# An expert-choice MoE and LoRA layer pair on one core: threshold search with seven candidates a step, one-hots built with a scalar per partition, and other work moved around them

## The reference

```python
w = weights[subjects]                              # layer 0, conditioning
flat_x = jnp.einsum('bct,bcd->bdt', x, w).reshape(N, D)
logits = flat_x @ Wg + bg
top_vals, top_idx = jax.lax.top_k(logits, 2)
probs = softmax(sparse top-2 logits)
for i in range(4):
    assigned = (top_idx == i).any(axis=-1)
    score = jnp.where(assigned, probs[:, i], -jnp.inf)
    sel_p, sel_idx = jax.lax.top_k(score, 1024)    # expert choice
    h = jax.nn.gelu(flat_x[sel_idx] @ W1[i], approximate=False)
    out = out.at[sel_idx].add(h @ W2[i] * sel_p[:, None])
x = x + out
x = x + layer1(x)        # silu(gate) * up with LoRA, down, then the scaled linear layer
```

## Time and profile before

| what | us |
|---|---|
| median of 3 runs (651.81 to 652.7) | 651.91 |
| the profiled execution, whole | 653.1 |
| its span in the trace | 651.3 |

### The profile page before, as it was taken

One profiled execution on the slowest core, in us unless ns is written; L12 is line 12 of the kernel. 1 busy time (PEld: TensorE's weight loads), 2 busy tenths in 40 slices (PEclk: granted clock), 3 DMA queues, 4 the chain that ended last, 5 costly groups with the idle time before them and its releaser, 6 DMA issues.

```text
span 651.3 us, 9696 instructions
## 1 busy us (share of the span) xinstructions
PE 605.0 (93%) x3323; PEld 503.4 (77%) x3323; DVE 382.1 (59%) x827; ACT 214.4 (33%) x448; POOL 132.6 (20%) x113
## 2 busy tenths in 40 slices
PE   4867389999999999979999999999999999999994
PEld 2735269999999999967888888888888888888883
DVE  7687867886786556505455545554555455545533
ACT  2435025764874755432212213122122131221110
POOL 4000040745453540652002003011030020000000
PEclk9979579999999999999999999999999999999997
DMA  8996329416329330831003104013031040120012
...
DMA packets 64219, 60.74 MB, mean 93 GB/s; under 512 B 37424, under 2 KB 56624, under 8 KB 62832
## 3 DMA queue, kind: packets, MB, share of 16 engines
...
...
## 4 chain that ended last, share of the span: by engine, by line
PE 86%; DVE 7%; DMA 2%; issue 1%; ACT 1%; POOL 0%; SPq 0%; ACTq 0%; DVEq 0%; POOLq 0%
PE bank L1081 23%; PE bank L1082 22%; PE bank L1083 22%; PE bank L1293 5%; PE bank L1262 3%; PE bank L1260 3%; DVE mix_row L668 2%; PE bank L1140 1%; PE bank L1114 1%; PE bank L1147 1%; PE bank L1194 1%; DVE onehot_r L831 1%; PE bank L1254 1%; DVE passed L780 1%; DVE passed_n L783 1%
## 5 line engine op out<-in xcount | busy, mean ns | idle before, releaser
L621 ACT ACTIVATE act<-bank 128x512 f32<-128x512 f32 x64 | 38.2, 598 | 229.9 <-PE bank L1293 229.9
L1046 DVE TENSOR_TENSOR prod<-bank,act 128x512 f32<-128x512 f32 x64 | 44.2, 690 | 99.6 <-PE bank L1293 99.6
L957 DVE TENSOR_TENSOR hid_lo<-hf,hid_hi 128x512 fp32r<-128x512 f32 (+1 forms) x72 | 45.4, 631 | 48.6 <-ACT hf L567 48.2
L1081 PE MATMUL bank<-w_hi,hid_hi 128*128 128x256 f32 x256 | 72.2, 282 | 0.0
L1082 PE MATMUL bank<-w_lo,hid_hi 128*128 128x256 f32 x256 | 72.1, 282 | 0.0
L1083 PE MATMUL bank<-w_hi,hid_lo 128*128 128x256 f32 x256 | 71.5, 279 | 0.0
L452 POOL DMA_INDIRECT x_rows<-y_sb,slot_row x32 | 53.7, 1678 | 65.9 <-ACT y_sb L554 58.9
L564 ACT ACTIVATE hid_hi<-bank 128x512 fp32r<-128x512 f32 (+1 forms) x72 | 39.8, 552 | 71.1 <-PE bank L1083 70.7
...
L1081 PE MATMUL bank<-xs_hi,w_hi 128*128 128x512 f32 (+1 forms) x144 | 54.7, 380 | 0.0
L1082 PE MATMUL bank<-xs_lo,w_hi 128*128 128x512 f32 (+1 forms) x144 | 53.2, 370 | 0.0
L1083 PE MATMUL bank<-xs_hi,w_lo 128*128 128x512 f32 (+1 forms) x144 | 53.2, 370 | 0.0
...
## 6 DMA issues: line engine op xcount, KB each, us to landing
...
xT<-in_xT SPq DMA_DIRECT2D x8, 512.0 KB, 8.5
x_sb<-in_x SPq DMA_DIRECT2D x8, 512.0 KB, 8.7
flat_rows<-flat_st SPq DMA_DIRECT2D x8, 512.0 KB, 5.5
outT<-out_sb SPq DMA_DIRECT2D x120, 32.0 KB, 1.6
...
```

Of the source, the lines that this page charges most:

```text
L621: act.activation(act1[h % 2][:, :], bank[h % 2][:, :], ACT.Silu).then_inc(silu1, 1)
L957: dve.tensor_tensor(lo[:, n], hf[s % 2][:, n], hi[:, n].bitcast(f32), ALU.subtract).then_inc(hid0, 1)
L1046: dve.tensor_tensor(prod[h % 2][:, :], bank[2 + h % 2][:, :], act1[h % 2][:, :], ALU.mult).then_inc(prod1, 1)
L1081: pe.matmul(out, lh, rh, start=start, stop=False, skip_group_check=True)
```

## The change

- **Masks and copies.** mix_row begins as a copy of adapter 0's matrix in place of the memset; seven predicated copies follow, and the z masks of quarters 0 and 1 stand between them, that of quarter 2 behind them, that of quarter 3 behind the copies into mix. PE's order of products, transposes and logits is changed to match.
- **Search.** Ten steps of three bits: seven candidates per expert. The comparison is two halves of 16 columns (448 elements each), each with its own count of asked. The sum over the columns on VectorE is gone: PE adds four slices of eight columns into one region of 224 columns, and VectorE sums the eight that are left, from PSUM.
- **Items.** Sixteen ahead of the search (twelve before), then two per step for eight steps and one per step for two; the last three folds come behind `route(0)`, in place of the eight fillers. WAIT_PARTS0 falls from 6 to 3.
- **ACT.** The casts of the first expert's weights to w_hi stand behind item 31 instead of item 22, and the Gelu table is loaded behind item 33.
- **One-hots.** onehot_r is written by eight tensor_scalars of 128 elements per quarter, each with a column of pos_r (now f32) as its scalar per partition. VectorE no longer waits for all items ahead of them (wdT has moved to other memory).

```diff
@@ -19,7 +19,8 @@
-SEARCH_STEPS = 15
+SEARCH_STEPS, SEARCH_BITS = 10, 3
+CAND = 2 ** SEARCH_BITS - 1
@@ -153,7 +154,7 @@
-        pos_r, pos_q = sb("pos_r", [P, E, G], bf16), sb("pos_q", [P, E, G], bf16)
+        pos_r, pos_q = sb("pos_r", [P, E, G], f32), sb("pos_q", [P, E, G], bf16)
@@ -179,9 +180,9 @@
-        cursor[0] = onehot_at
+        cursor[0] = offset_of["xs1_hi"]
...
-        assert cursor[0] <= late_at
+        assert cursor[0] <= hid_at
@@ -210,10 +211,10 @@
-        cand = sb("cand", [P, E, 3], f32)
-        passed = sb("passed", [P, E, 3, G], bf16)
-        passed_n = sb("passed_n", [P, E, 3], bf16)
-        kept = [sb(f"kept{i}", [P, E, 4], f32) for i in range(2)]
+        cand = sb("cand", [P, E, CAND], f32)
+        passed = sb("passed", [P, E, CAND, G], bf16)
+        passed_n = sb("passed_n", [P, E, CAND], f32)
+        kept = [sb(f"kept{i}", [P, E, CAND + 1], f32) for i in range(2)]
@@ -311,8 +312,7 @@
-        ROWS_BEFORE_SPLITS = 22
-        ROWS_FIRST = 12
+        ROWS_FIRST, FOLDS_LATE = 16, 3
@@ -327,7 +327,7 @@
-        WAIT_GATHER, WAIT_ROWS, WAIT_PARTS0, WAIT_X1 = 8, 2, 6, 40
+        WAIT_ROWS, WAIT_PARTS0, WAIT_X1 = 2, 3, 40
@@ -528,14 +528,14 @@
                 last.then_inc(item_ev, 1)
-                if n == ROWS_BEFORE_SPLITS:
+                if n == ITEMS - FOLDS_LATE - 1:
+                    act.activation(warm[:, :], cols[:, 0:1], ACT.Gelu)
+                if n == G - 1:
...
                             act.activation(hi[:, a, :], r[:, a, :], ACT.Copy).then_inc(hi0, 1)
-            act.activation(warm[:, :], cols[:, 0:1], ACT.Gelu)
...
             def slots_hi(b, k, src):
@@ -663,13 +663,6 @@
             dve.tensor_tensor(subj_is[:, :, :], adapter_of, over(adapter_id, G), ALU.is_equal)
-            link(dve.memset(mix_row[:, :, :], 0.0))
-            for a in range(NAD):
-                link(dve.copy_predicated(mix_row[:, :, :], over(subj_is[:, a, :], 32),
-                                         subj_w[:, a, :].unsqueeze(1).to_broadcast([P, G, 32])))
-            dve.memset(ones_b[:, :], 1.0).then_inc(mix_rows, 1)
-            dve.wait_ge(pack2_in, 16)
...
             def z_masked(q):
@@ -678,17 +671,32 @@
-            for q in range(3):
-                z_masked(q)
-            dve.tensor_copy(rank[:, :, :], behind)
-            dve.tensor_copy(before_b[:, :], before)
-            dve.tensor_copy(iota_b[:, :], iota)
-            dve.memset(kept[0][:, :, 3], 0.0)
-            z_masked(3)
+            def mix_of(a):
...
+                link(dve.copy_predicated(mix_row[:, :, :], over(subj_is[:, a, :], 32),
+                                         subj_w[:, a, :].unsqueeze(1).to_broadcast([P, G, 32])))
...
+            link(dve.tensor_copy(mix_row[:, :, :], subj_w[:, 0, :].unsqueeze(1).to_broadcast([P, G, 32])))
+            for a in range(1, 4):
+                mix_of(a)
+            z_masked(0)
+            for a in range(4, 6):
+                mix_of(a)
+            z_masked(1)
+            for a in range(6, NAD):
+                mix_of(a)
+            dve.memset(ones_b[:, :], 1.0).then_inc(mix_rows, 1)
+            z_masked(2)
             dve.wait_ge(zeroed, 3)
...
                 dve.tensor_copy(mix[r, :, r], mix_row[r, :, :]).then_inc(mixed, 1)
+            z_masked(3)
+            dve.wait_ge(pack2_in, 16)
+            dve.tensor_copy(rank[:, :, :], behind)
+            dve.tensor_copy(before_b[:, :], before)
+            dve.tensor_copy(iota_b[:, :], iota)
+            dve.memset(kept[0][:, :, CAND], 0.0)
             dve.wait_ge(logit_tr, 1)
@@ -773,22 +781,22 @@
+            counts = bank[7][:, 0:E * CAND * 8].rearrange("p (e j g) -> p e j g", e=E, j=CAND)
             for i in range(SEARCH_STEPS):
                 now, then = kept[i % 2], kept[(i + 1) % 2]
-                link(dve.tensor_tensor(cand[:, :, :].bitcast(u32), over(now[:, :, 3].bitcast(u32), 3),
-                                       steps[:, i, :].unsqueeze(1).to_broadcast([P, E, 3]), ALU.bitwise_or))
-                link(dve.tensor_tensor(passed[:, :, :, :], score[:, :, :].unsqueeze(2).to_broadcast([P, E, 3, G]),
-                                       over(cand[:, :, :], G), ALU.is_ge))
-                with nc.allow_low_precision("counts up to 32"):
-                    dve.tensor_reduce(passed_n[:, :, :], passed[:, :, :, :], AX.X, ALU.add).then_inc(asked, 1)
-                if i % 3 == 0 and i < 12:
-                    part = done(prob_parts(i // 3))
+                link(dve.tensor_tensor(cand[:, :, :].bitcast(u32), over(now[:, :, CAND].bitcast(u32), CAND),
+                                       steps[:, i, :].unsqueeze(1).to_broadcast([P, E, CAND]), ALU.bitwise_or))
+                for half in range(2):
+                    g = slice(half * G // 2, (half + 1) * G // 2)
+                    dve.tensor_tensor(passed[:, :, :, g], score[:, :, g].unsqueeze(2).to_broadcast([P, E, CAND, G // 2]),
+                                      over(cand[:, :, :], G // 2), ALU.is_ge).then_inc(asked, 1)
+                if i % 2 == 0 and i < 8:
+                    part = done(prob_parts(i // 2))
                 dve.wait_ge(counted, i + 1)
-                link(dve.scalar_tensor_tensor(now[:, :, 0:3], bank[7][:, 0:3 * E].rearrange("p (e j) -> p e j", j=3),
-                                              float(CAP), cand[:, :, :], ALU.is_ge, ALU.mult))
-                link(dve.tensor_reduce(then[:, :, 3], now[:, :, :], AX.X, ALU.max))
-            thr = kept[SEARCH_STEPS % 2][:, :, 3]
...
+                link(dve.tensor_reduce(passed_n[:, :, :], counts, AX.X, ALU.add))
+                link(dve.scalar_tensor_tensor(now[:, :, 0:CAND], passed_n[:, :, :], float(CAP), cand[:, :, :], ALU.is_ge, ALU.mult))
+                link(dve.tensor_reduce(then[:, :, CAND], now[:, :, :], AX.X, ALU.max))
+            thr = kept[SEARCH_STEPS % 2][:, :, CAND]
@@ -818,7 +826,6 @@
             places(slice(0, 1))
-            dve.wait_ge(item_ev, ITEMS)
@@ -828,8 +835,9 @@
                                   vals[:, e, g, :].unsqueeze(2).to_broadcast([P, n, Q, C]), ALU.mult)
-                dve.tensor_tensor(onehot_r[:, g, :], over(pos_r[:, e, g], P),
-                                  iota_b[:, :].unsqueeze(1).to_broadcast([P, n, P]), ALU.is_equal).then_inc(route_in, 1)
+                for i in range(g.start, g.stop):
+                    last = dve.tensor_scalar(onehot_r[:, i, :], iota_b[:, :], pos_r[:, e, i:i + 1], None, ALU.is_equal)
+                last.then_inc(route_in, 1)
@@ -1116,16 +1124,21 @@
-            for i in range(8):
+            for i in range(4):
                 z_products(i)
-                if i in (3, 5):
-                    z_by_token(i // 2 - 1)
-            z_by_token(2)
+            z_by_token(0)
+            z_products(4)
             pe.wait_ge(blocks_in, 1)
             logits(0)
+            z_products(5)
+            z_by_token(1)
+            z_products(6)
+            z_by_token(2)
+            logits(1)
+            z_products(7)
+            logits(2)
             z_by_token(3)
-            for q in range(1, 4):
-                logits(q)
+            logits(3)
             pe.wait_ge(logit_ev, 1)
@@ -1156,14 +1169,18 @@
             for i in range(SEARCH_STEPS):
-                pe.wait_ge(asked, i + 1)
-                pe.matmul(bank[7][:, 0:3 * E], ones_b[:, :], passed_n[:, :, :].rearrange("p e j -> p (e j)"),
-                          start=True, stop=True).then_inc(counted, 1)
-                for _ in range(2 if i < 6 else 3 if n < G else 1):
-                    if n < ITEMS:
-                        item(n)
-                        n += 1
-            assert n == ITEMS
+                for half in range(2):
+                    pe.wait_ge(asked, 2 * i + half + 1)
+                    for t in range(2):
+                        g = slice((2 * half + t) * 8, (2 * half + t + 1) * 8)
+                        last = pe.matmul(bank[7][:, 0:E * CAND * 8], ones_b[:, :],
+                                         passed[:, :, :, g].rearrange("p e j g -> p (e j) g"),
+                                         start=half == 0 and t == 0, stop=half == 1 and t == 1, skip_group_check=True)
+                last.then_inc(counted, 1)
+                for _ in range(2 if n < G else 1):
+                    item(n)
+                    n += 1
+            assert n == ITEMS - FOLDS_LATE
             pe.wait_ge(ranks_in, 1)
@@ -1195,10 +1212,11 @@
             route(0)
+            for n in range(ITEMS - FOLDS_LATE, ITEMS):
+                item(n)
             pe.wait_ge(ident_in, 1)
...
             pe.wait_ge(item_ev, ITEMS)
-            keep_busy(WAIT_GATHER, bank[2], w1)
             for k in range(KD):
```

8 lines of the change are left out of this document (4 added, 4 removed).

## The result

| kernel | median us | lowest to highest, runs | time over before, 95 % interval |
|---|---|---|---|
| before | 652.7 | 651.81 to 654.81, 7 | 1 |
| changed | 649.63 | 648.81 to 651.05, 7 | 0.995 (0.9935 to 0.9964) |

The changed kernel is 0.5 % faster. Its profiled execution took 648.81 us (span 647.0), that of before 653.1 (span 651.3): 4.3 us between the two profiles, 3.1 between the medians. The profiled execution of the changed kernel is the fastest of its seven, so the profiles show more gain than the medians.

The account below looks back on a forecast made before the run. Serial preparation up to about 92 us bounds the kernel, then PE is busy without a gap. Terms -2.6 + 0.1 + 1.0 - 1.1 - 0.5 = -3.1 us give 648.8 us, range 645.8 to 652.1.

Parts of the forecast that it names:

- The new step: Search: one step of the new form takes 2.71 us, ten 27.1, against fifteen at 2.05, 30.8.
- Logits: Before the search: reordered masks and copies bring the logit to 24.1, 2.6 us earlier, a gain the store wait hides.
- The wait that takes over: Search: PE waits at item 20 for the first store; step 4 at 47.65, search end 63.95, -2.6 us.
- the bound of 1.2 us: Search, store wait: if PE's clock is still high at 43.9, 1.2 us better.
- a rival: Search: no wait for the store, ten steps plus 0.75 for one long candidate instruction, 643.9 us; chance 0.04.
- The rival that is slower than before: PE's clock stays low through steps 4 to 9, a step takes 2.9 us, whole 653.5; chance 0.10.
- Ranks: End of the search: the fold of step 9 holds the rank matmuls back by 0.1 us.
- One-hots: After the search: eight tensor_scalars at 0.17 us replace one 1.13 us instruction per quarter, +1.0 us for four.
- The rival of 0.11: One-hots: the scalar's load is hidden, 0.11 us per one-hot, 2.0 us better, 646.8; chance 0.20.
- Gather wait: Before the first product: three folds replace eight fillers, take 6.4 us with the last copy, and are covered by the gathers.
- the -1.1 of the fillers: Behind the gather wait: three fillers instead of six end before xs_lo is ready, -1.1 us.
- The clock at the products: First products: PE stays busy from the route on, so its clock is high when they begin, -0.5 us.

Follow-up runs that it names:

- e6: Changed kernel with VectorE comparing in one instruction and adding the 32 columns itself, twelve rows ahead of the search: 654.02 us, 1.0012 of before.
- e4: Changed kernel with masks, copies to mix_row and PE's logits in the order of before: 649.99 us, 0.9969 of before.
- e9: Changed kernel with the first four stores ahead of the expert's weights and the logits' last masks and transposes reordered: 646.96 us, 0.9906 of before.
- e1: Changed kernel with the one-hots written as before, one tensor_tensor per quarter: 648.41 us, 0.9933 of before.
- e10: Changed kernel with the first four stores ahead of the expert's weights and six fillers behind the transposes instead of three: 648.8 us, 0.9939 of before.
- e5: Changed kernel with the old fifteen-step search, twelve rows ahead, all folds in it and eight gather-wait fillers: 652.98 us, 0.9993 of before.

## Why the prediction was right, point by point

The changed kernel was forecast at 648.8 us and took 649.63, with a ratio that stands for 3.3 us less than before; 3.1 less was forecast. In part that is luck: the logit missed by 2.9 us at no cost, and two errors nearly cancelled, step 4 of the search 0.7 us earlier than forecast and the gather wait 0.6 longer.

**The new step**: 2.71 forecast, 2.71 measured, at the high clock and with no wait for the store. The terms were right one by one, and e6 shows that the sum over eight partial counts in place of the long reduce is what makes the change pay.

**Logits**: wrong, and it didn't matter. Forecast 24.1, measured 27.03. The failed step is "behind the last copy come two masks and two quarters instead of four": right in count, but no price stands beside it. The last copy was put near 20, which leaves 4.1 us for the two masks and quarters; it ended at 20.94, and they took 6.1. A quarter has 16 records and takes 1.6 to 1.9 us, and the last quarter's transposes were not ready but stood behind the third quarter on PE. xT also came some 0.8 us later in this execution (PE's second tile at 9.90 after 9.10). e4 and e9 bear it out: old order 26.62, another tail 25.66.

**The wait that takes over**: the mechanism was right, the code's wait and the one row at 43.46 were enough to find it. Its size was off twice. The store landed at 43.97 instead of 43.4, and PE had stood for 1.7 us instead of over 4, since the search started 3 us later than forecast and its step 0 had the long row; the clock was high, which I had put as the bound of 1.2 us. So step 4 began at 46.91 instead of 47.65. e4 has the low clock, and with the store's 0.6 it gives the forecast number: 47.65 + 0.6 = 48.25, measured 48.19. The reason that I gave for the low clock, PE's idle time, is not shown: in e4 the clock was low before PE stood still. That the hole hides the start of the search was right too: start at 34.20 and not at 31.2, end at 63.18 and not at 63.95. In e9, where no store stands in the way, an earlier logit does arrive at the end.

**The long row.** I left out that GpSimd's multiplication holds up VectorE for 1.1 us inside the search, although show one cand of 923 ns, and I used that number only in a rival. In the changed kernel it lay ahead of the store's wait, so it hardly counted.

**The clock in the search.** I took the steps before and behind the hole as 2.71 throughout. But the clock fell inside the search in most kernels, and a step with two rows then took 2.90 (in the changed kernel step 1, from 37.99 to 40.89, with the clock low from 39.1 on; in e1 steps 5 and 6, with 0.50 in 50 to 54). The rival that is slower than before had 2.9 for such a step, so its price was right; the six steps that it asked for did not come; it was three at most in the kernels with the new search (e6, where VectorE adds, apart).

**Ranks**: +0.1 forecast; from the end of the search to the first onehot_q 3.57 us instead of 3.45.

**One-hots**: 0.17 us forecast for one, 0.1625 measured. Eight are 1.30 and not 1.38, against 1.13 before, so +0.17 a quarter and +0.65 in all, forecast +1.0 (8 x 0.17 is 1.36 and not the 1.38 of the forecast, a slip of 0.1 in the four). The rival of 0.11 falls. How much of the 0.1625 is the scalar is argued and not shown; a row of 128 f32 elements with immediates speaks for the 0.06. It gives way after 0.15, the one with a scalar in the earlier trace rows after 0.21 (timeline of VectorE, changed kernel):

```profile
30.02 0.23 DVE L755 TENSOR_SCALAR unused<-rank 128x128 f32<-128x128 f32 x1
30.17 0.18 DVE L757 SCALAR_TENSOR_TENSOR t_g<-t_g,t_g 128x32 f32<-128x32 f32 x1
```

By the Trainium skill (Vector Engine (DVE) Microarchitecture Reference, Measured stream behaviour on trn2), which gives about 75 ns per instruction beside its elements and names no price for a scalar, it would have been 0.11, an estimate with my 0.03 for the elements. The trace does not agree with that sum.

**Gather wait**: half of it came. Folds and copy took 7.55 us and not 6.4, because the clock rose 4.7 us behind the first fold and not 3.2; so the copy of the last fold, not the gathers, let the transposes begin. The first product came 11.65 us behind the first fold, forecast 11.1. Of the -1.1 of the fillers -0.5 was left: from the first onehot_q to the first product 20.23 us against 20.11 before, with 0.65 more of one-hots in it. The 1.1 was itself rounded up: by its rows it is 90.10 - 89.06 = 1.04, and no product starts the moment xs_lo is ready. And e10 shows that six fillers are free at the high clock, so this term holds at the low clock only; e5, with three fillers at the low clock, has it (20.03, 0.65 of one-hots included: -0.7).

**The clock at the products**: -0.5 forecast; at the first hid_lo the lead is 0.5 larger than at the first product. The reason held as well (1.00 in 84 to 92 us).

**Sum** at the first hid_lo: search end -3.36, ranks +0.12, one-hots +0.65, gather wait -0.53, clock -0.5: -3.6, forecast -3.1. The profiled span is 0.7 better still; 0.6 of it is a shorter wait for the rows read back ahead of layer 1 (2.2 us, before 2.8), which the other runs show to scatter from 2.1 to 2.7. That wait is also what the prediction overlooked when it took PE as busy without a gap from 92 us on.
